# Second attention: two score products in a row, then two transposed ones, where one and one took turns

## The reference, cut to what matters

```python
q = (input_tensor @ wq.T + bq).reshape(B, S, H, D).transpose(0, 2, 1, 3)   # B 8, S 512, H 16, D 16
k = (input_tensor @ wk.T + bk_).reshape(B, S, H, D).transpose(0, 2, 1, 3)
v = (input_tensor @ wv.T + bv).reshape(B, S, H, D).transpose(0, 2, 1, 3)
scores = jnp.einsum('bhsd,bhtd->bhst', q, k) / jnp.sqrt(jnp.float32(D))
attn = jax.nn.softmax(scores, axis=-1)
out = jnp.einsum('bhst,bhtd->bhsd', attn, v)
out = out.transpose(0, 2, 1, 3).reshape(B, S, E) @ wo.T + bo
```

## Time and profile before

| | us |
|---|---|
| median of 3 runs | 2075.05 (2073.18 to 2085.74) |
| the profiled execution | 2076.42 |
| its span in the trace | 2074.7 |
| second attention, first to last `score_t` | 1459.3 to 2051.8 |
| one row b of it (4 groups), from `split_ot` to `split_ot` | 76.2 |

### The profile page before, as it was taken

The page is one execution under the profiler, slowest core; times in us unless marked ns, Lnnn a source line. Parts: engine busy times, 40 slices in busy tenths (PEclk is TensorE's granted clock), DMA queues, the critical chain, the costliest instruction groups (busy, mean ns, idle before and its releaser), DMA issues. The chain is left out here.

```text
span 2074.7 us, 39084 instructions
## 1 busy us (share of the span) xinstructions
PE 1898.8 (92%) x12080; PEld 1467.4 (71%) x12080; DVE 1441.9 (69%) x2916; ACT 1293.3 (62%) x3069; POOL 646.3 (31%) x1021
## 2 busy tenths in 40 slices
PE   1999999998999999999999789994999999999997
PEld 1887878778878888788888578873556656655653
DVE  5785885876858858858678554434777777777773
ACT  3675674665756756747557465542686776777784
POOL 0353453543533534525435213222001011011112
PEclk9999999999999999999999999996899999999999
DMA  6110211111111111111111383412001011011001
GB/s 224 42 42 25 49 42 33 41 32 42 42 32 42 42 31 47 39 43 37 27 41 42 100 299 112 138 35 98 21 1 52 0 51 51 0 51 51 0 31 41
DMA packets 75758, 112.35 MB, mean 54 GB/s; under 512 B 8256, under 2 KB 49600, under 8 KB 75072
## 3 DMA queue, kind: packets, MB, share of 16 engines
q1 hardware_dynamic: 75040, 109.14, 17.9%
q10 hardware_dynamic: 544, 1.05, 0.2%
HBM read 55.64 MB, written 20.97 MB: 37 GB/s over the span
## 5 line engine op out<-in xcount | busy, mean ns | idle before, releaser
L1537 DVE TENSOR_REDUCE nm<-ps 128x1 f32<-128x512 f32 x512 | 336.9, 687 | 116.2 <-PE ps L1396 112.1
L1648 ACT ACTIVATE pt<-pst 128x512 f32<-128x512 f32 x512 | 296.1, 602 | 142.4 <-PE pst L1404 141.2
L808 POOL TENSOR_SCALAR pr<-pr,rinv 128x128 f32<-128x128 f32 (+3 forms) x512 | 263.9, 536 | 374.6 <-DVE rinv L694 374.6
L573 ACT ACTIVATE pr<-sc,nmax 128x128 f32<-128x128 f32 (+3 forms) x512 | 268.4, 527 | 142.5 <-DVE nmax L683 141.1
L683 DVE TENSOR_REDUCE nmax<-sc 128x1 f32<-128x128 f32 (+3 forms) x512 | 222.7, 483 | 72.8 <-PE sc L408 72.7
L814 POOL TENSOR_TENSOR qk<-ra,rb 128x256 f32<-128x256 f32 x256 | 183.4, 738 | 219.7 <-DVE rb L705 187.5
L1396 PE MATMUL ps<-kb,qb 96*128 96x512 f32 x512 | 239.2, 470 | 12.2 <-DVE nm L1537 9.9
L1404 PE MATMUL pst<-qb,kb 128*128 128x512 f32 x512 | 208.2, 408 | 6.7 <-ACT pt L1648 3.4
L1396 PEld LDWEIGHTS ps<-kb,qb 96*128 96x128 f32 x512 | 98.4, 193 | 143.7 <-DVE nm L1537 94.9
L420 PE MATMUL w<-ident,pr 128*128 128x128 f32 x1280 | 169.3, 279 | 26.3 <-DVE rb L705 20.4
L382 PE MATMUL w<-wq_hi,xt_hi 128*128 128x384 f32 x512 | 183.7, 359 | 3.7 <-DVE pt L690 2.2
(11 more groups left out here) (205 smaller groups left out, 4568.2 us busy)
## 6 DMA issues: line engine op xcount, KB each, us to landing
k<-k SPq DMA_DIRECT2D x256, 128.0 KB, 2.2
raw<-in_w SPq DMA_DIRECT2D x16, 640.0 KB, 5.9
raw<-in_w SPq DMA_DIRECT2D x8, 704.0 KB, 4.3
xa<-in_x SPq DMA_DIRECT2D x2, 2048.0 KB, 13.8
x<-in_x SPq DMA_DIRECT2D x8, 512.0 KB, 3.7
x_scratch<-x SPq DMA_DIRECT2D x8, 512.0 KB, 3.5
xt_hi_scratch<-xt_hi SPq DMA_DIRECT2D x1, 4096.0 KB, 13.1
xt_lo_scratch<-xt_lo SPq DMA_DIRECT2D x1, 4096.0 KB, 23.0
```

Of the source, the lines that this page charges most:

```text
L573: act.activation(pr[:, h, SOFF[i]:SOFF[i] + (i + 1) * P], sc[:, bank, at:at + (i + 1) * P], ACT.Exp, bias=nmax[:, h, i:i + 1], accum_out=r ...
L808: pool.tensor_scalar(p, p, rinv[:, h, i:i + 1], 1.0, ALU.mult, ALU.mult).then_inc(scaled, 1)
L1537: dve.tensor_reduce(nm[:, g % 2, i, h:h + 1], ps[:, i % 2, :], AXX, ALU.max, negate=True).then_inc(max_done, 1)
L1648: act.activation(pt[:, g % 2, h, i, :], pst[:, i % 2, :], ACT.Exp).then_inc(exp_done, 1)
```

## The change

In `group`, the PE program's loop over i handles two tiles at once: at even i it issues `score` i, `score` i + 1, `score_t` i, `score_t` i + 1; at odd i it issues none of them. All else stays at its place (h, i), behind what the loop issues there. DVE's, ACT's and POOL's programs are as they were, and so are all waits, banks and numbers of instructions.

```diff
                     for h in range(HG):
                         for i in range(NT):
-                            if h < HG - 1 and more1:
-                                score(q + 1, (g + 1) % NG1, h + 1, i)
-                            elif h == HG - 1 and more2:
-                                score(q + 2, (g + 2) % NG1, 0, i)
-                            score_t(q, g, h, i)
+                            if i % 2 == 0:
+                                for n in (i, i + 1):
+                                    if h < HG - 1 and more1:
+                                        score(q + 1, (g + 1) % NG1, h + 1, n)
+                                    elif h == HG - 1 and more2:
+                                        score(q + 2, (g + 2) % NG1, 0, n)
+                                for n in (i, i + 1):
+                                    score_t(q, g, h, n)
                             if (h, i) in TURNS and more2:
```

## The result

The change took 2124.57 us (2123.58 to 2130.9, 4 runs) against 2074.52 for the kernel before: ratio 1.024, interval 1.0204 to 1.0277, so 50 us slower. The forecast was 2120. The profiled execution took 2123.58 us.

The account below looks back on a forecast made before the run. PE was taken as the bound on the whole, though with waits for DVE and ACT. Terms of 6.1 us a row made 37 over six rows; row 7 about 3.5, row 0 about 5: +45, forecast 2120, range 2094 to 2137.

Parts of the forecast that it names:

- head 0, groups 0 and 1: First transposed score stands behind a second score waiting for DVE's late maximum; ACT's chain then delays the last: +0.64 each.
- head 0, group 2: Second score and second transposed score run under the first `turn_z`'s wait for `split_ot`: -0.27 us.
- head 1, four times: All groups: last score waits for DVE's maximum 1, last transposed score for ACT's exponential 1: +0.63 us each.
- head 2, groups 0, 2, 3: DVE sets the pace; third transposed score now comes behind the last score, so `weigh` is later: +0.22 us each.
- head 2, group 1: Last score waits for maximum 1 behind `take_proj` 1, and `project` 3 waits behind `project` 2: +1.36 us.
- head 3, groups 0 and 3: Next head's first score waits for DVE behind `take_n` anyway, so the moved products lie under that wait: 0.
- head 3, group 1: The `turn_on` stand side by side: +0.1 us.
- head 3, group 2: `out_project` 3 comes to wait for DVE's `take_out` 1, which is behind `take_n`: +0.26 us.
- Rows 0 and 7: Row 0, lacking `turn_o`, `out_project`, `split_ot` and starting at half clock: about 5 us; row 7, with less work: about 3.5.
- No change, since the waits lie under others: Rival: added waits lie under existing ones, DVE and ACT have time to spare; 2060 to 2096 us, chance 0.13.
- Hidden loads: Rival: second of each pair finds its weights loaded, at most 27 us saved, 2049 us; chance 0.05.
- The clock: Rival: stalls let PE's granted clock fall from 2.4 to 1.2 GHz now and then, 2140 to 2160 us; chance 0.04.

Follow-up runs that it names:

- first half alone: Against the changed kernel, only tiles 0 and 1 of each head paired, tiles 2 and 3 one and one: 2097.03 us, ratio 1.0091.
- moving one copy: ACT's copy to `ou` one tile later: 2116.96 us in the changed kernel, 2067.24 us in the kernel before.
- half maxima: DVE's maximum over the first 256 of 512 columns: 2058.97 us in the kernel before, 2096.61 us in the changed kernel.
- moving three: Changed kernel with ACT's three copies to `kb` in head 1 each one tile later: 2114.98 us, ratio to before 1.0192.
- taking all holds off: Changed kernel with DVE's maxima over 256 columns and ACT's copies to `ou` and `kb` one tile later: 2077.82 us, ratio to before 1.0007.
- head 3 alone: Against the changed kernel, tiles paired only in head 3 of each group: 2079.36 us, ratio to the kernel before 1.0021.

## Why the prediction was right

Its sum was +45 us on the profiled execution and +47 was seen (2076.42 to 2123.58). The mechanism was the one that it named, but that the sums lie so close is partly luck: six rows were 0.4 too cheap each, and row 0 was 1.3 too dear. The terms a row, predicted and measured:

| step | predicted | measured |
|---|---|---|
| head 0, groups 0 and 1: T0 behind a gated S1, ACT's chain 0.64 later | 0.64 each | 0.59 each |
| head 0, group 3 | 0.23 | 0.23 |
| head 0, group 2: the wait for `split_ot` filled | -0.27 | -0.30 |
| head 1, four times: S3 held by DVE, then T3 by ACT | 0.63 each | 0.60 to 0.62 |
| head 2, groups 0, 2, 3 | 0.22 each | 0.23, 0.24, 0.24 |
| head 2, group 1 | 1.36 | 1.47 |
| head 3, groups 0 and 3 | 0 | 0 |
| head 3, group 1 | 0.1 | 0.26 |
| head 3, group 2 | 0.26 | 0.48 |
| a row | 6.1 | 6.5 |

Head 3 of groups 1 and 2 was sized too small. In group 1 S3 now waits for maximum 1 until 1.88, with T2 and `turn_on` behind it, which used to fill that time. In group 2 I had only `out_project` 3 behind DVE's `take_out` 1, and took DVE's own times as unmoved. They move. DVE's `take_out` 0, before at 1739.79 - 1738.31 = 1.48 from S0, comes at 1762.07 - 1760.12 = 1.95, since `out_project` 0 now stands behind S1, T0 and T1; all that follows in DVE's program, `take_n` and `take_out` 1 with it, is that much later, and `out_project` 3 waits for it. First before, then changed, where the last line is `out_project` 3:

```profile
1739.79 0.42 DVE L1576 TENSOR_TENSOR so<-w1a,bo_sb 128x256 f32<-128x256 f32 x1 [0.25 <-PE w1a L1450]
```

```profile
1762.07 0.42 DVE L1579 TENSOR_TENSOR so<-w1a,bo_sb 128x256 f32<-128x256 f32 x1 [0.72 <-PE w1a L1450]
...
1765.04 0.38 PE L1448 MATMUL w1a<-wo_hi,ot_hi 128*128 128x256 f32 x1 [0.23 <-DVE so L1579]
```

The run with the first half alone agrees: it has the whole 0.46 of it. In head 2 of group 1 the prediction ended maximum 1 at 4.35, though its own terms add up to 2.62 + 1.14 + 0.69 = 4.45; the trace has 4.33, because the record of the maximum begins 0.09 before that of `take_proj` ends. Rows 0 and 7 came at 3.7 and 3.3 (predicted 5 and 3.5).

Of its signs, T0 at 0.95, S3 at 1.88, T3 at 2.7 and a row of 82.7 came as written, and PE was busy 487 of 510 us, 95.5%, from 1520 to 2030 us. ACT's idle time ahead of exponentials, waiting for `pst`, grew by 40 us, from 141.2 to 180.8, a little less than the sum.

Step by step: that ACT's chain holds T3 in head 0 is shown by moving one copy (0.31 and 0.36 back, with pairs and without); that DVE's maximum starts that delay agrees with the half maxima, under which group 0 loses 0.33 there instead of 0.59; that head 1 is ACT's as much as DVE's by moving three (0.36 of 0.62), by the half maxima, which change nothing there, and by taking all holds off (0.05 left); that head 2 of group 1 is its own stall by unpairing it (1.47 back). That head 3 of groups 0 and 3 neither loses nor gives back is shown by head 3 alone.

The rivals. "No change, since the waits lie under others" fails because a head of PE ends with `weigh` and the next S0 follows at once in fourteen of sixteen heads: only head 3 of groups 0 and 3 has slack, and there the loss is indeed 0. "Hidden loads" fails since the gates bind: where a score is held, its load waits with it; and with all three holds off, head 1 still isn't under 3.95. The rule that the prediction took from the Trainium skill, "Perfetto Trace Analysis", Optimizing Tensor Performance, Matmuls, that groups rotate through banks, would have said no change against the 2.4% measured; the order of the banks is not what counts here but which product stands behind a bank that is still being emptied. The clock stayed: the profiled runs were granted 0.977 before and after, and 1.00 from 1520 to 2030 us.

What remains argued and not tried: how head 0's 0.59 and head 1's remaining 0.26 divide between DVE's maximum and the later T0; each follows from the timeline, but no run took one without the other at full work.

## What to carry to other kernels

With two consumers and two banks each, try alternating the products first: when one must wait, the other consumer's product has already gone. Grouping like with like puts a blocked product ahead of a free one on an engine that starts in order; count, for each place, what stands behind the product that waits, transpositions for a third engine included. PE at 97% busy says nothing against such a loss: walk one period from start to start and add the gates.

## What the runs showed of the hardware that I had not expected

- A faster consumer returns little of the loss: with maxima of 0.42 us instead of 0.69 a row lost 5.5 instead of 6.5 us. In head 2 it returned nothing, since ACT became the gate there, and it loses 0.24 to 0.25 as before.
- The reports of idle time of the weight loads, 83.2 us for DVE in the change and 78.6 before, hardly move although 47 us were lost; ACT's grow from 8.9 to 30.4. Together that is 26 us: the distance from start to start shows the whole loss, the list of waits about half.
- Time ahead of anything changed (the stage's first score) moved between 1435 and 1442 us from trace to trace, as much as several of the effects sought here; periods inside one trace agreed to 0.02 to 0.04 us.
